# A selective scan with a gated MLP on one core: six states instead of four on the token route, eleven instead of ten C products on GpSimd, and a new order of all engines

## The reference

```python
xz = x @ W_xproj.T                      # 64 dt columns, 16 of B, 16 of C
dt = softplus(xz[:64] @ W_dt.T + b_dt)
dA = exp(dt * -exp(A_log))              # per channel and state
dBx = dt * B * x                        # per channel and state
h_t = dA_t * h_(t-1) + dBx_t            # along the 1024 tokens
y_t = sum over the states of h_t * C_t
x1 = layernorm(x + y + Dp * x)
hid = silu(x1 @ wg.T) * (x1 @ wu.T)     # 768 hidden, int weights / 127
out = layernorm(x1 + hid @ wd.T)
```

## Time and profile before

| | |
|---|---|
| median of 3 runs | 2022.97 us (2020.72 to 2024.86) |
| the profiled execution | 2022.87 us, its span 2021.1 us |
| mean granted TensorE clock | 0.947 of 2.4 GHz |
| busy | DVE 1869.1 us (92%), POOL 1768.4 (87%), PE 1729.2 (86%), ACT 1474.9 (73%), PEld 1339.9 (66%) |
| HBM | 203.87 MB read, 18.87 MB written, 110 GB/s |

### The profile page before, as it was taken

The page is one execution under the profiler, slowest core; times in us unless marked ns, Lnnn a source line. Parts: engine busy times, 40 slices in busy tenths (PEclk is TensorE's granted clock), DMA queues, the critical chain, the costliest instruction groups (busy, mean ns, idle before and its releaser), DMA issues.

```text
span 2021.1 us, 35597 instructions
## 1 busy us (share of the span) xinstructions
PE 1729.2 (86%) x10664; PEld 1339.9 (66%) x10664; DVE 1869.1 (92%) x2317; ACT 1474.9 (73%) x2668; POOL 1768.4 (87%) x811
## 2 busy tenths in 40 slices
PE   5688888888889888889888889888889888889887
PEld 3566676666677666777666776666766666766665
DVE  5899999999999999999999999999999999999993
ACT  6767777777777778777677877777777778776752
POOL 5998889988988988988988899989889989889970
PEclk7899999999999999999999999999999999999989
DMA  7234333233333233333234233234233243232300
GB/s 248 95 98 137 104 119 116 86 123 135 105 117 115 83 126 131 105 105 125 89 126 130 96 110 120 100 126 131 95 110 113 96 136 121 99 115 88 112 12 21
DMA packets 102675, 223.18 MB, mean 110 GB/s; under 512 B 9617, under 2 KB 44018, under 8 KB 102642
## 3 DMA queue, kind: packets, MB, share of 16 engines
q1 hardware_dynamic: 102642, 222.78, 33.3%
HBM read 203.87 MB, written 18.87 MB: 110 GB/s over the span
## 4 chain that ended last, share of the span: by engine, by line
PE 49%; issue 15%; ACT 14%; DVE 13%; POOL 7%; DVEq 1%; ACTq 0%; POOLq 0%; DMA 0%; SPq 0%
PE p_o L997 16%; PE p_y L960 13%; PE p_m L984 6%; POOL h L416 5%; DVE h L707 4%; DVE hid L743 3%; DVE h L699 3%; ACT p_da L533 3%; PE p_m L908 3%; PE p_c L937 3%; PE p_m L900 3%; ACT da_k L533 2%; ACT res_n L576 2%; PE p_da L928 2%; DVE silu_g L737 2%
## 5 line engine op out<-in xcount | busy, mean ns | idle before, releaser
L406 POOL TENSOR_TENSOR ub<-u,b_bc 128x1024 f32<-128x1024 f32 x384 | 906.1, 2375 | 0.1
L416 POOL TENSOR_TENSOR h<-h,c_bc 128x1024 f32<-128x1024 f32 x320 | 757.0, 2378 | 0.0
L533 ACT ACTIVATE p_da<-dt,neg_a 128x512 f32<-128x512 f32 x768 | 524.1, 686 | 231.2 <-DVE h L699 229.2
L960 PE MATMUL p_y<-ident,h 128*128 128x128 f32 x4096 | 566.2, 290 | 36.9 <-POOL h L416 36.7
L960 PEld LDWEIGHTS p_y<-ident,h 128*128 128x128 f32 x4096 | 509.7, 150 | 87.0 <-POOL h L416 52.0
L699 DVE TENSOR_TENSOR_SCAN h<-p_da,h_carry,ub 128x512 f32<-128x512 f32 x384 | 474.5, 1266 | 9.2 <-ACT p_da L533 8.3
L699 DVE TENSOR_TENSOR_SCAN h<-p_da,ub 128x512 f32<-128x512 f32 x384 | 452.4, 1208 | 15.0 <-ACT p_da L533 9.3
L997 PE MATMUL p_o<-wt_down,hid 128*128 128x256 f32 x1536 | 352.3, 379 | 3.0 <-DVE res L750 1.6
L997 PEld LDWEIGHTS p_o<-wt_down,hid 128*128 128x128 f32 x1536 | 284.4, 190 | 52.2 <-issue 14.7
L984 PE MATMUL p_m<-x_t,wt_up 128*128 128x512 f16 x744 | 194.3, 384 | 81.1 <-DVE hid L743 81.1
L707 DVE TENSOR_TENSOR h<-h,p_c 128x1024 f32<-128x1024 f32 x192 | 229.9, 1197 | 25.3 <-PE p_c L937 25.3
(11 more groups left out here) (101 smaller groups left out, 1875.7 us busy)
## 6 DMA issues: line engine op xcount, KB each, us to landing
b_bc<-bc_rows_dram SPq DMA_DIRECT2D x128, 768.0 KB, 4.0
c_bc<-bc_rows_dram SPq DMA_DIRECT2D x320, 256.0 KB, 4.2
x_in<-in_L_attn_x SPq DMA_DIRECT2D x32, 512.0 KB, 3.5
out_x<-res_n SPq DMA_DIRECT2D x32, 512.0 KB, 3.0
bc_rows_dram<-bc_rows SPq DMA_DIRECT2D x32, 64.0 KB, 1.6
hid<-in_L_ffn_w_gate SPq DMA_DIRECT2D x1, 768.0 KB, 4.9
hid<-in_L_ffn_w_up SPq DMA_DIRECT2D x1, 768.0 KB, 6.8
res<-in_L_ffn_w_down SPq DMA_DIRECT2D x1, 384.0 KB, 7.2
```

Source lines behind the costliest of these rows:

```text
L406: nc.gpsimd.tensor_tensor(ub[:, i % UB_SLOTS, :, :], u[:, par, :, :], b_bc[:, i:i + 1, :].broadcast_to([P, DH, T]), ALU.mult).then_inc(s_u ...
L416: nc.gpsimd.tensor_tensor(h[:, s % H_SLOTS, :, :], h[:, s % H_SLOTS, :, :], c_bc[:, i:i + 1, :].broadcast_to([P, DH, T]), ALU.mult).then_i ...
L533: nc.scalar.activation(da, dt[:, par, q, :], ACT.Exp, scale=neg_a[:, q, s:s + 1]).then_inc(s_da, 1)
L960: ins = nc.tensor.matmul(p_y_tok[:, k, q * P:(q + 1) * P], h[:, s % H_SLOTS, q, k * P:(k + 1) * P], ident[:, :], start=False, stop=(s == S ...
```

## The change

Constants and the table of the order are new. The token route takes six states (2, 5, 8, 10, 12, 15), so that ten remain in `B_STATES` (0, 1, 3, 4, 6, 7, 9, 11, 13, 14), with five `ub` slots. These ten have their decays in `p_da`, the six in `da_k`. `POOL_STATES` has eleven states, and DVE multiplies by C for five: 1, 6, 7, 13, 15. The sums come a step earlier (lag 3 for POOL's states, 2 for DVE's), u*B on POOL is three steps ahead instead of four. The rows of B are loaded in six runs between the token states, (0,1), (3,4), (6,7), (9), (11), (13,14), instead of four of three states each. The functions of the engines are the same but for the run that `times_b` waits for.

```diff
-POOL_STATES = (0, 1, 2, 3, 4, 7, 8, 9, 10, 11)
-UB_AHEAD = 4
+POOL_STATES = (0, 2, 3, 4, 5, 8, 9, 10, 11, 12, 14)
+UB_AHEAD = 3
-SUM_LAG = {True: 4, False: 3}
+SUM_LAG = {True: 3, False: 2}
...
-    "x_transposed": (2, 1), "x_out": (2, 1), "project": (3, 0), "rank_out": (4, 1), "bc_out": (4, 1),
-    "project_dt": (4, 1), "softplus_abs": (5, 1), "softplus_exp": (6, 0), "softplus_log": (6, 1),
-    "dt_of": (7, 1), "u_of": (7, 1),
-    "u_transposed0": (12, 1), "u_out0": (15, 0), "u_transposed1": (15, 0), "u_out1": (15, 1),
-    "z_out": (4, 0), "stats1": (4, 2), "mean1": (5, 1), "norm_inputs": (7, 0), "scalars": (5, 0), "norm1": (7, 0),
-    "x1_transposed": (7, 2), "x1_high": (8, 0), "x1_low": (9, 0),
-    "gate_up": (9, 1), "tanh": (9, 0), "silu": (10, 0), "hidden": (10, 1),
-    "down0": (0, 1), "down1": (1, 0), "down2": (1, 1), "down3": (1, 2),
-    "down4": (3, 0), "down5": (3, 2), "down6": (4, 0), "down7": (4, 1),
-    "residual0": (2, 2), "residual1": (6, 0), "stats2": (6, 0), "mean2": (6, 1), "norm2": (10, 1),
-    "bc_turned": (7, 1), "bc_cols": (9, 1),
+    "x_transposed": (1, 0), "x_out": (1, 1), "project": (2, 1), "rank_out": (3, 0), "bc_out": (3, 0),
+    "project_dt": (3, 0), "softplus_abs": (4, 0), "softplus_exp": (4, 1), "softplus_log": (5, 0),
+    "dt_of": (5, 2), "u_of": (8, 0),
+    "u_transposed0": (8, 2), "u_out0": (14, 0), "u_transposed1": (15, 1), "u_out1": (15, 0),
+    "z_out": (2, 0), "stats1": (3, 2), "mean1": (4, 0), "norm_inputs": (6, 1), "scalars": (6, 1), "norm1": (7, 1),
+    "x1_transposed": (8, 0), "x1_high": (8, 0), "x1_low": (9, 0),
+    "gate_up": (9, 2), "tanh": (9, 0), "silu": (10, 0), "hidden": (10, 1),
+    "down0": (0, 0), "down1": (0, 0), "down2": (0, 1), "down3": (1, 1),
+    "down4": (2, 1), "down5": (2, 2), "down6": (2, 2), "down7": (3, 0),
+    "residual0": (1, 1), "residual1": (4, 1), "stats2": (5, 0), "mean2": (5, 0), "norm2": (11, 1),
+    "bc_turned": (6, 0), "bc_cols": (7, 1),
...
-K_STATES = (3, 7, 11, 15)
+K_STATES = (2, 5, 8, 10, 12, 15)
-UB_SLOTS = 6
+UB_SLOTS = 5
...
+    B_RUNS = [[s for s in B_STATES if sum(k < s for k in K_STATES) == r] for r in range(NK)]
...
-            def broadcast_b(c, k, par):
+            def broadcast_b(c, r, par):
+                first, last = B_RUNS[r][0], B_RUNS[r][-1]
+                i, n = B_STATES.index(first), last + 1 - first
                 if not (isinstance(c, int) and c == 0):
-                    wait(sp, s_ub, NB * (c - 1) + (k + 1) * B_GROUP)
...
+                    wait(sp, s_ub, NB * (c - 1) + i + n)
+                sp.dma_start(b_bc[:, i:i + n, :], bc_dram[par:par + 1, first:last + 1, :].broadcast_to(
+                    [P, n, T])).then_inc(s_b[r], 16)
...
                     broadcast_b(c + 1, 0, 1 - par)
                     broadcast_b(c + 1, 1, 1 - par)
+                    broadcast_b(c + 1, 2, 1 - par)
                     broadcast_c(c + 1, 0, 1 - par)
-                    broadcast_b(c + 1, 2, 1 - par)
+                    broadcast_b(c + 1, 3, 1 - par)
+                    broadcast_b(c + 1, 4, 1 - par)
                     broadcast_c(c + 1, 1, 1 - par)
                 if last:
                     store(c - 2)
                 if nxt:
-                    broadcast_b(c + 1, 3, 1 - par)
+                    broadcast_b(c + 1, 5, 1 - par)
                     broadcast_c(c + 1, 2, 1 - par)
...
-                pool.wait_ge(s_b[s // GROUP], 16 * (c + 1))
+                pool.wait_ge(s_b[sum(k < s for k in K_STATES)], 16 * (c + 1))
```

More of the change, by code:

```diff
@@ L75, in mamba_ffn_block @@
     NB = N - NK
-    B_GROUP = NB // NK
-    assert K_STATES == tuple(range(GROUP - 1, N, GROUP)) and B_GROUP == GROUP - 1
+    B_RUNS = [[s for s in B_STATES if sum(k < s for k in K_STATES) == r] for r in range(NK)]
+    assert K_STATES[-1] == N - 1 and all(B_RUNS)
     assert NB % UB_SLOTS == N % H_SLOTS == NK % K_SLOTS == 0
@@ L81, in mamba_ffn_block @@
     SUM_ORDER = sorted(range(N), key=lambda s: (sum_at[s], s))
-    assert all(sum_at[s] < N or s not in POOL_STATES for s in range(N))
+    assert N - 1 not in POOL_STATES
     x_chunks = x.rearrange("b (h k p) d -> (b h) p k d", p=P, k=TT)
@@ L199, in mamba_ffn_block @@
         s_rows_dram = sem("s_rows_dram")
-        s_b = [sem(f"s_b{k}") for k in range(N // GROUP)]
+        s_b = [sem(f"s_b{r}") for r in range(NK)]
         s_ut_ps = sem("s_ut_ps")
@@ L334, in rows_out @@
                 sp.wait_ge(s_rows_dram, 16 * (c + 1))
-            def broadcast_b(c, k, par):
+            def broadcast_b(c, r, par):
+                first, last = B_RUNS[r][0], B_RUNS[r][-1]
+                i, n = B_STATES.index(first), last + 1 - first
                 if not (isinstance(c, int) and c == 0):
-                    wait(sp, s_ub, NB * (c - 1) + (k + 1) * B_GROUP)
-                sp.dma_start(b_bc[:, k * B_GROUP:(k + 1) * B_GROUP, :],
-                             bc_dram[par:par + 1, k * GROUP:k * GROUP + B_GROUP, :].broadcast_to(
-                                 [P, B_GROUP, T])).then_inc(s_b[k], 16)
+                    wait(sp, s_ub, NB * (c - 1) + i + n)
+                sp.dma_start(b_bc[:, i:i + n, :], bc_dram[par:par + 1, first:last + 1, :].broadcast_to(
+                    [P, n, T])).then_inc(s_b[r], 16)
             def broadcast_c(c, k, par):
@@ L352, in _ @@
             rows_out(0, 0)
-            for k in range(N // GROUP):
-                broadcast_b(0, k, 0)
-                broadcast_c(0, k, 0)
+            for r in range(NK):
+                broadcast_b(0, r, 0)
+                if r < N // GROUP:
+                    broadcast_c(0, r, 0)
             def step(c, par, batch, nxt, core, prev, last):
```

## The result

The changed kernel takes 1999.88 us (1997.66 to 2004.38, 4 runs), the kernel before 2022.48 in the same comparison: a ratio of 0.9889, 95% interval [0.9877, 0.9901]. It is faster by 22.6 us (1.1%), where I had forecast 54: the time lies in my range of 1934 to 2012, but less than half of the forecast gain came. The profiled execution has a span of 1995.8 us.

A forecast was written before the change was run, and what follows sets the result against it. DVE was taken as the bound. Its work of 57.05 us plus idle 2.2 gave a period of 59.25, 1.67 less a chunk; 52 us over 31 chunks and 2 at the end made 1969 us (own range 1950 to 1990, overall 1934 to 2012).

The forecast's parts named there:

- p_da from PE: DVE's idle time for PE's transposes into p_da: 0.45 x 6/4 = 0.68 us a chunk, since six states take that way.
- decays: DVE's idle time for decays: 0.4 us a chunk as before, fewer of them but ACT fuller.
- tanh: DVE's wait for the tanh of a gate tile: 0.7 us a chunk, for a low PE clock before the gates.
- p_c: DVE's wait for PE's transposes into p_c: 0.25 us a chunk left, where it was 0.63.
- eight of 0.65: PE at a chunk's start, steps 0 to 3: eight down products counted at 0.65 us each.
- some 16.5 us in 13.5: PE, steps 0 to 3: some 16.5 us of work in 13.5 us, ending at 16.9 us of the chunk.
- half a us to spare at state 5: PE's transposes for state 5, which DVE needs in p_da at 18.1 us: ready about half a us early.
- rival B: PE takes POOL's place, late from its crowd at a chunk's start: idle 3.5, period 60.55, 2010 us; chance 0.20.
- every token state waits: Part of rival B: the spare time at state 5 is negative and DVE waits at all token states; idle 3.5 us.
- rival C: PE's low clock after its emptiness lasts into the gates: idle 5.3, period 62.35, slower at 2065 us; chance 0.12.
- Start and end: Outside the steady chunks: end 2 us shorter (p_c wait of 1.10 and a sum of 0.9 go), start 0 within 3.
- stop before rstd: Sign in the profile after: POOL stands near 6 us a chunk before rstd (59.25 - 52.9).

The follow-up runs named there:

- down_half: The changed kernel with the down product taking three of its six hidden blocks, so its output isn't the reference's; 1917.53 us, ratio 0.9485 to the kernel before.
- thin_act: The changed kernel with waits that can't be late taken from ACT, so its loop has fewer instructions; 1998.24 us, ratio 0.9882 to the kernel before.

## Why the prediction was right and wrong

*Loads: right.* DVE 56.73 us a chunk (forecast 57.05), PE 54.6 (54.5), ACT 48.7 (49.4), POOL 53.2 (52.9). The idle time was not: 3.78 in place of 2.2. By term, in us a chunk: p_da from PE 2.10 (forecast 0.68), decays 0.77 (0.4; ACT's stall is in it), residual 0 0.44 (no term), x1_low 0.35 (no term), tanh 0.02 (0.7), p_c none (0.25), unnamed 0.1 (0.2).

*"eight of 0.65": the step that failed.* A down job is 1.30 us, so "some 16.5 us in 13.5" was 21.5. The error is one of reading: I had counted half of the 48 records of 0.216 us that a chunk's down products are, where the row of L997 above had all of them. down_half took just this term out and the wait with it: 82 us. My half a us to spare at state 5 was a lack of 2.18, and that place is the one I named for rival B: idle 3.78 (3.5 there) and a period of 60.51 (60.55). B's 2010 us was the nearer time; its chance of 0.20 was too low by this same term. B's reading in general, "every token state waits", was not so: only state 5 does.

*The scaling of the p_da waits: wrong as well.* I took 0.45 x 6/4 = 0.68, as if each token state had a share. But the earlier trace rows has 28 of these waits in 28 chunks, so one a chunk, and the timeline puts it at state 3, the first token state of the chunk:

```profile
1066.58 2.51 DVE L699 TENSOR_TENSOR_SCAN h<-da_k,h_carry,p_da 128x512 f32<-128x512 f32 x2 [0.29 <-PE p_da L928]
```

The wait depended on where a token state stands behind PE's crowd of work, not on how many there are: 61.0/29 = 2.10 us a chunk came in place of 0.68. Residual 0 (12.9/29 = 0.44) hangs on the same down jobs and had no term of its own in the sum.

*The waits that go: right, by more than said.* p_c and tanh fell to nothing (0.25 and 0.7 forecast). For tanh the way I laid it out holds: rival C, the low clock reaching the gates, did not happen. PE stood 3.65 us before state 8 (forecast 4), and what followed ran slow, as four transposes of 1.12 us in the same timeline, where it is 0.60 at full clock; but it ended before the gates, which begin at 1019.60 in this chunk (first granted clock, then PE's timeline, below). In all 31 chunks the granted clock was back at 1.00 between 0.8 and 3.6 us ahead of the first gate. Only x1_low paid, 10.2/29 = 0.35 us a chunk, and over the chunks this wait goes with the clock: where it was back at 1.00 at least 1.8 us ahead of this instruction (six chunks) DVE didn't wait, where it was back 1.1 us ahead or less it waited 0.5. My 0.7 for the clock stood at the wait for tanh; what it cost came here.

```profile
1013.00:1015.00 2.00, 2.00 (x9) 1.20 (x8) 2.00 (x3) 2.00 (x6) 2.00 (x2) 0.50 0.00 0
1018.00:1020.00 2.00, 1.61 (x14) 1.18 (x12) 2.00 (x3) 2.00 (x5) 1.47 (x1) 1.00 0.00 0
```

```profile
1015.00 1.12 PE L941 MATMUL p_c<-ident,bc_t 128*128 128x128 f32 x4
```

*Not in the sum: the fetches.* They made DVE wait 0.62 us a chunk before state 1, but only behind a pass of the loop: 13 waits of 1.24 us, 16 us in all (the 19 of my expectations took all 31 chunks). Removing them gave 0.7 to 2.2 us in three pairs, since PE was late behind them. So they took little of the missing gain.

*The eleventh C product.* I counted DVE's 1.12 us. It also lets PE begin its down jobs at hidden 5 instead of after a product of DVE. The forecast had that in its layout without saying so, and in this order it is worth more than the product (56 of 103 us).

*Start and end.* For the end I had -2, and it is -3.7 behind the last scan: the wait of 1.10 us is gone; the rest I take for the fewer sums that trail, without a run for it. For the start I had 0, within 3, and that was wrong: the first two chunks are 5.6 us shorter, 4.6 more than at the steady rate, and no run looks at why. Here I had luck, for without this the gain would have been smaller still.

*POOL.* Its stop before rstd is 75.0/29 = 2.6 us, not the 6 I gave as a sign; it stands 116.0/29 = 4.0 us a chunk for ACT's copies into `h_carry` instead. POOL's load is as forecast, and DVE never waits for it in this window.

The account of the span (2021.1 to 1995.8, by starts of first scans): the first two chunks took 111.7 us where they had taken 117.3, the 29 next 1753.1 where it was 1767.3 (0.49 each), the last 56.7 for 58.5, and what follows the last scan 48.3 for 52.0. In the steady stretch DVE's load fell by 1.44 us a chunk and its idle time grew by 1.02, which leaves 0.42. I had 1.67 a chunk there.

## What to carry to other kernels

When work is laid out by hand, take the cost of each piece from a row of its own, and hold the sum of an engine's pieces against its busy time in the window: a term at half its size leaves a gap there, here 5.2 of 53.2 us. Count how often a wait comes in a chunk before scaling it with the number of states. In a kernel of in-order engines, look for the longest stretch in which one engine never stops, and for the first thing another engine wants from its end; moving that date, and what stands ahead of the next one, gave 46.6 us on top of the 22.6 of the change. A wait that is removed shows what it had covered: here softplus behind state 5, and residual 0 behind a stall of ACT.

## What the runs showed of the hardware

Whether a loop's instructions were fetched again depended on where it begins: of ACT's 310 instructions a pass some were fetched anew each pass, with a stall of 2.1 to 2.3 us, in one place, and none 60 instructions further on; in passes of 288 (the kernel before) and 282 (thin_act) none were either, and those loops also begin elsewhere. The profile shows it as an idle ACT released by "issue" and as packets of kind instruction (82 against 15 to 17).
